# A language-model tower with a two-way state-space block: the convolution's third tap shared between VectorE and TensorE, the projections computed in plain FP32, and the fills of TensorE's order placed anew

## The reference

```python
h = emb[x]
Q, K, V = (heads(wq, bq), heads(wk, bk), heads(wv, bv))      # p = h @ w + b
...
xz = x @ in_w.T
xh, z = jnp.split(xz, 2, axis=-1)
xp = jnp.pad(xh, ((0, 0), (D_CONV - 1, 0), (0, 0)))
xc = conv_b + sum((xp[:, k:k + L, :] * conv_w[:, k] for k in range(D_CONV)))   # D_CONV = 4 taps
xc = jax.nn.silu(xc)
proj = xc @ xproj_w.T
delta = jax.nn.softplus(dt @ dt_w.T + dt_b)
deltaA = jnp.exp(jnp.einsum('bld,dn->bldn', delta, A))
deltaBu = jnp.einsum('bld,bln->bldn', delta * xc, Bm)
h = dA * h + dBu                                             # the scan over time
y = jnp.einsum('bdn,bn->bd', h, c)
y = (y + xc * D_param) * jax.nn.silu(z)
return y @ out_w.T
```

## Time and profile before

| | |
|---|---|
| time, median of 3 runs | 3424.03 us (3408.75 to 3426.32) |
| the profiled execution | 3430.8 us |
| its span in the profile | 3429.0 us |
| TensorE busy (PE) | 3235.7 us, 94% |
| VectorE busy (DVE) | 2913.3 us, 85% |
| ScalarE busy (ACT) | 2734.0 us, 80% |
| GpSimd busy (POOL) | 1449.0 us, 42% |

### The profile page before, as it was taken

The page is one execution under the profiler, slowest core; times in us unless marked ns, Lnnn a source line. Parts: engine busy times, 40 slices in busy tenths (PEclk is TensorE's granted clock), DMA queues, the critical chain, the costliest instruction groups (busy, mean ns, idle before and its releaser), DMA issues. The chain is left out here.

```text
span 3429.0 us, 75632 instructions
## 1 busy us (share of the span) xinstructions
PE 3235.7 (94%) x26913; PEld 2179.4 (64%) x26913; DVE 2913.3 (85%) x2894; ACT 2734.0 (80%) x4665; POOL 1449.0 (42%) x1379
## 2 busy tenths in 40 slices
PE   8599999999999999977899999999999999998898
PEld 7233333333333333336799999999999999986665
DVE  4789999999979999824599999999999999999422
ACT  3078888888878888842799999999999999999344
POOL 3100000000000000000588899998888899899200
PEclk9589999999989999988999999999999999999999
DMA  8420312112020200033111121211111111112431
GB/s 221 86 26 5 43 18 30 24 23 35 11 42 6 38 9 5 5 81 111 39 51 63 63 69 63 69 51 63 63 63 63 66 66 63 57 45 99 143 116 55
DMA packets 94154, 192.81 MB, mean 56 GB/s; under 512 B 16804, under 2 KB 31940, under 8 KB 92296
## 3 DMA queue, kind: packets, MB, share of 16 engines
q1 hardware_dynamic: 82616, 174.28, 18.5%
q10 hardware_dynamic: 9680, 9.84, 0.9%
q0 software_dynamic: 1536, 4.20, 0.8%
HBM read 136.64 MB, written 51.12 MB: 55 GB/s over the span
## 5 line engine op out<-in xcount | busy, mean ns | idle before, releaser
L1258 POOL TENSOR_TENSOR m_g<-m_hs,m_cb 128x512 f32<-128x512 f32 x1024 | 1286.0, 1287 | 175.5 <-PE m_ps_y L1290 89.8
L608 DVE TENSOR_REDUCE a_mx<-a_ps_m 128x2 f32<-128x1024 f32 x1024 | 1241.5, 1223 | 85.9 <-PE a_ps_m L466 68.4
L584 ACT ACTIVATE a_probs<-a_ps_s 128x512 f32<-128x512 f32 x2048 | 1110.5, 596 | 200.1 <-PE a_ps_s L496 156.0
L1390 DVE TENSOR_TENSOR_SCAN m_hs<-m_da,m_carry,m_ps_x 128x512 f32<-128x512 f32 x768 | 930.2, 1263 | 19.8 <-issue 8.0
L466 PE MATMUL a_ps_m<-a_k,a_q 48*128 48x512 f32 x2048 | 774.9, 471 | 35.6 <-DMA a_q<-q_scr 21.2
L496 PE MATMUL a_ps_s<-a_q,a_k 50*128 50x512 f32 x2048 | 774.7, 458 | 7.7 <-ACT a_probs L584 2.9
L1347 ACT ACTIVATE m_da<-m_delta,m_a_cur 128x512 f32<-128x512 f32 x1024 | 715.2, 713 | 0.0
L503 PE MATMUL a_ps_o<-a_probs,a_v 128*32 128x256 f32 x8192 | 669.0, 399 | 8.5 <-ACT a_o L571 8.0
L1278 PE MATMUL m_ps_x<-m_ident,m_bu 128*128 128x128 f32 x4096 | 627.6, 276 | 50.5 <-DVE m_hs L1390 32.1
L1290 PE MATMUL m_ps_y<-m_ident,m_g 128*128 128x128 f32 x4096 | 616.2, 273 | 0.6 <-POOL m_g L1258 0.6
L1332 ACT ACTIVATE m_bu<-m_dut,m_bt 128x512 f32<-128x512 f32 x832 | 593.8, 714 | 15.1 <-PE m_ps_x L1278 14.8
(11 more groups left out here) (150 smaller groups left out, 2525.6 us busy)
## 6 DMA issues: line engine op xcount, KB each, us to landing
m_cb<-c_scr SPq DMA_DIRECT2D x128, 512.0 KB, 3.7
y_scr<-m_ysb SPq DMA_DIRECT2D x16, 1024.0 KB, 6.5
ffn_y<-y_scr SPq DMA_DIRECT2D x14, 1024.0 KB, 7.4
a_k<-k_scr SPq DMA_DIRECT2D x96, 128.0 KB, 6.6
a_q<-q_scr SPq DMA_DIRECT2D x96, 128.0 KB, 8.9
q_scr<-p_partsq SPq DMA_DIRECT2D x16, 512.0 KB, 3.9
k_scr<-p_partsk SPq DMA_DIRECT2D x16, 512.0 KB, 6.3
m_xn<-xn_scr SPq DMA_DIRECT2D x16, 512.0 KB, 5.0
```

The lines of the kernel that those rows point to most:

```text
L584: nc.scalar.activation(probs[:, t % PR, HEADS[j]], turned(i), ACT.Exp, scale=float(DK) ** -0.5).then_inc(exped, 1)
L608: nc.vector.reduce_max(mx[:, i:i + wide], ps_m[:, b:b + wide], AX.X).then_inc(m_maxed, 1)
L1258: nc.gpsimd.tensor_tensor(g[:, t % NG], hs[:, t % NHS], cb[:, quarter % 2, n % CQ], ALU.mult).then_inc(g_ok, 1)
L1390: nc.vector.tensor_tensor_scan(hs[:, t % NHS, rev], da[:, t % NDA, rev], ps_x[:, t % NX, rev], carry[:, n, i:i + 1] if p else 0.0, ALU.mul ...
```

## The change

Two things are changed in the projections. Products are no longer split: the weights and `p_hT` stay FP32, Q and K are 4 matmuls each and V is 8 in a chunk, and the two parts of weights and of `p_hT` and what made them (lines 209, 238 and 243) are gone. And the loop is a loop again: TensorE transposes a chunk, waits for ScalarE's copy, and does Q, K and V; it no longer turns chunk n + 1 between K and V of chunk n.

In the state-space block, channel tiles 0 and 2 keep the third tap on VectorE, and for tiles 1 and 3 TensorE does it: their CONV fills have 12 matmuls in place of 8, and VectorE's in-place instruction is left out for them. The tap matrices are 24 in place of 16. All the tables of slots are written anew.

```diff
-WEIGHT_STEPS = [(0, 0, 0), (0, 0, 1), (1, 0, 0), (1, 0, 1), (0, 1, 0), (0, 1, 1)]
...
-        w_parts = [sb(f"p_wp{n}", [P, PARTS, KD, D], F32R) for n in "qkv"]
-        hT = sb("p_hT", [P, 2, PARTS, KD, CH], F32R)
+        hT = sb("p_hT", [P, 2, KD, CH], FP32)
...
+                for b, c, n, buf in chunks(pe):
+                    pe.wait_ge(rows_in[buf], (n - buf) * 32 + 64)
                     pe.wait_ge(ht_ok, ONE + n)
                     for t in range(4):
                         for k in range(KD):
                             last = nc.tensor.transpose(ps_t[:, k, t * P:(t + 1) * P],
                                                        rows[:, buf, t, k * P:(k + 1) * P], ident[:, :])
...
                     pe.wait_ge(ht_ok, ONE + n + 1)
                     for a in range(2):
                         pe.wait_ge(parts_ok[a], ONE + n)
                         for m in range(KD):
-                            last = products(ps_qk[a][:, m], lambda i, k: w_parts[a][:, i, k, m * P:(m + 1) * P],
-                                            lambda i, k: hT[:, buf, i, k], WEIGHT_STEPS)
+                            for k in range(KD):
+                                last = nc.tensor.matmul(ps_qk[a][:, m], w_sb[a][:, k, m * P:(m + 1) * P],
+                                                        hT[:, buf, k], start=k == 0, stop=k == KD - 1)
                         last.then_inc(mm_done[a], 1)
-                    if n + 1 < B * NC:
-                        turned(n + 1)
...
             def _(act):
...
+                for b, c, n, buf in chunks(act):
                     act.wait_ge(ht_ps, ONE + n + 1)
+                    nc.scalar.activation(hT[:, buf], ps_t[:, :, :], ACT.Copy).then_inc(ht_ok, 1)
...
+VECTOR_TAP = (0, 2)
...
-        taps = sb("taps", [P, 2, ND, DC - 2, P], FP32)
+        taps = sb("taps", [P, 2, ND, DC - 1, P], FP32)
...
-                 CONV + 2: (-17, -17, -17, -17, -17, -17, -17, -15), CONV + 3: (-15, -15, -15, -15, -15, -15, -15, -15),
+                 CONV + 3: (-14, -14, -14, -13, -13, -13, -13, -13, -13, -13, -13, -13),
...
-                back = k + 2
+                back = k + (2 if dt in VECTOR_TAP else 1)
...
+            if dt in VECTOR_TAP:
+                before = HB + 1 if z else HB - 1
+                nc.vector.scalar_tensor_tensor(out=ps_a[:, f % NA], in0=xh[:, dt, before:before + CH], scalar=conv_w[:, z, dt, DC - 2:DC - 1],
+                                               in1=ps_a[:, f % NA], op0=ALU.mult, op1=ALU.add).then_inc(tapped, 1)
+                nc.vector.wait_ge(tapped, s * len(VECTOR_TAP) + VECTOR_TAP.index(dt) + 1)
...
-                    for tap in range(DC - 2):
+                    for tap in range(DC - 1):
```

More of the change, by code:

```diff
@@ L144, in _ @@
                 identity(nc.gpsimd, ident[:, :], cleared, ident_ok)
-                pool.wait_ge(ids_ok, ONE + 1)
-                for n in range(B * NC):
-                    buf = n % 2
-                    if n >= 2:
-                        pool.wait_ge(ht_ps, ONE + n - 1)
-                    nc.gpsimd.tensor_copy(ids_c[:, buf], ids_t[:, n * 4:n * 4 + 4]).then_inc(ids_copied, 1)
+                for b, c, n, buf in chunks(pool):
+                    pool.wait_ge(rows_free, ONE + n + 1)
+                    pool.wait_ge(ids_ok, ONE + 1)
+                    nc.gpsimd.tensor_copy(ids_c[:, buf], ids_t[:, bass.ds(n * 4, 4)]).then_inc(ids_copied, 1)
                     pool.wait_ge(ids_copied, ONE + n + 1)
+                    pool.nop(nofuse=True)
                     for t in range(4):
@@ L171, in turned @@
                                                        rows[:, buf, t, k * P:(k + 1) * P], ident[:, :])
-                    last.then_inc(ht_ps, 1)
-                def products(out, stationary, moving, steps):
-                    for i, (part_s, part_m, k) in enumerate(steps):
-                        last = nc.tensor.matmul(out, stationary(part_s, k), moving(part_m, k), start=i == 0, stop=i == len(steps) - 1)
-                    return last
-                pe.wait_ge(ids_ok, ONE + 1)
-                turned(0)
-                pe.wait_ge(w_low, ONE + 3)
-                for n in range(B * NC):
-                    buf = n % 2
+                            if t == 3 and k == KD - 1:
+                                last.then_inc(ht_ps, 1)
+                    pe.wait_ge(ht_ps, ONE + n + 1)
+                    pe.sem_inc(rows_free, 1)
                     pe.wait_ge(ht_ok, ONE + n + 1)
@@ L188, in _ @@
                         for m in range(KD):
[L189 to L190 removed]
+                            for k in range(KD):
+                                last = nc.tensor.matmul(ps_qk[a][:, m], w_sb[a][:, k, m * P:(m + 1) * P],
+                                                        hT[:, buf, k], start=k == 0, stop=k == KD - 1)
                         last.then_inc(mm_done[a], 1)
[L192 to L193 removed]
                     pe.wait_ge(v_ok, ONE + n)
                     for t in range(4):
[L196 to L197 removed]
+                        for k in range(KD):
+                            last = nc.tensor.matmul(ps_v[:, t], hT[:, buf, k, t * P:(t + 1) * P], w_sb[2][:, k],
+                                                    start=k == 0, stop=k == KD - 1)
                     last.then_inc(v_mm, 1)
@@ L234, in _ @@
                 nc.vector.tensor_copy(ids_t[:, :], ps_t[:, 0, 0:NI]).then_inc(ids_ok, 1)
-                def turned_low(n):
-                    dve.wait_ge(ht_high, ONE + n + 1)
-                    nc.vector.tensor_tensor(hT[:, n % 2, 1], ps_t[:, :, :], hT[:, n % 2, 0].bitcast(FP32), ALU.subtract).then_inc(ht_ok, 1)
                 dve.wait_ge(w_in, ONE + 96)
-                for w in range(3):
-                    dve.wait_ge(w_high, ONE + w + 1)
-                    nc.vector.tensor_tensor(w_parts[w][:, 1], w_sb[w][:, :, :], w_parts[w][:, 0].bitcast(FP32), ALU.subtract).then_inc(w_low, 1)
-                turned_low(0)
-                for n in range(B * NC):
-                    b, c, buf = n // NC, n % NC, n % 2
+                for b, c, n, buf in chunks(dve):
                     for a in range(2):
```

63 lines of the change are left out of this document (24 added, 39 removed).

## The result

The kernel after took 3437.4 us in the median (3420.6 to 3460.3), against 3416.8 for the kernel before in the same comparison: ratio 1.0067, 95% interval 1.0051 to 1.0083. By the ratio that is 23 us slower, 17 to 28; the two medians lie 20.6 us apart.

What follows compares the result with a forecast made beforehand. VectorE and TensorE, both nearly full, were taken to bound the state-space step, TensorE the projections. Terms 23.5 + 1.6 + 2.0 + 3.9 = +31.0 us gave a median of 3455 us, range 3430 to 3476.

Steps and rivals of the forecast that it cites:

- The case that I held likeliest: Whole kernel: the forecast's own case, a median between 3445 and 3465 us, chance 0.52.
- Projections, +23.5: Projections: a chunk takes 12.52 us for 9.27, +22.75 from first K to last, and the first K ends 0.7 later.
- Tap matrices, +1.6: Building the tap matrices: eight more at 0.20 us on VectorE, all on the path since TensorE waits, +1.6 us.
- First two convolutions, +2.0: Two convolutions ahead of the stream: VectorE waits for TensorE tile by tile, +2.0 us, between 0 and 3.6.
- The stream, +3.9: The other 14 state-space steps: +0.23 us in each of ten, +0.4 in each of four without carry, +3.9 us.
- The sum of stretches: State-space step: TensorE's time in slots where it has more to do plus VectorE's elsewhere, 95.7 us before, 96.0 after.
- The sign that I named for the step: State-space step: VectorE's idle time ahead of scans in slots 50 to 8 grows by 1.5 to 2 us.
- the other signs: Profile after: Q to Q 12.5 us, TensorE idle some 1.1 us before Q, 32 third-tap instructions left.
- VectorE stays the bound: State-space step: TensorE takes the added matmuls into its gaps, 21.6 us won, +5.5 in all, 3430 us; chance 0.20.
- TensorE becomes the bound all through: State-space step: TensorE's added matmuls all count, 25.1 us lost, +52.2 in all, 3476 us; chance 0.15.
- The tables fit better: State-space step: new slots bring it to TensorE's 92.5 us plus 0.4, 46 us won, 3405 us; chance 0.05.
- Attention's clock: Attention's start: full 2.4 GHz at once would win up to 24 us, 3431; a longer 1.2 GHz stretch costs; chance 0.08.

## Why the prediction was right, and where it wasn't

**Time.** 3455 was forecast. The ratio puts the kernel at 3447 from the 3424.0 that the forecast started from, +23 us where +31.0 was forecast; the profiled execution was forecast at 3461.8 and took 3455.7. The case that I held likeliest (3445 to 3465) is the one that happened, by a narrow margin: the ratio's interval gives 3441 to 3452, and the median of the kernel's own executions is 3437.4. For the block its mechanism was wrong. By the marks the four terms are 24.6 + 1.6 + 3.6 - 8.6 = +21.2 us: the first two hold, the third is short by what the tables cost there, and the stream's has the wrong sign and is what the sum is too high by. The two last errors, 1.6 us too little and 12.5 too much, partly cancel. Of the 24.9 us between the profiled executions the other 3.7 lie in stretches without changed work, and that they are so few is luck: attention alone differs by up to 28 us between traces with the same work.

**Projections, +23.5.** Measured +24.6. Chunk to chunk 12.57 us for 12.52; an FP32 instruction of 512 columns (27.71 - 24.28) / 8 = 0.43, as taken from the feed-forward block; copy and hand-overs 1.11 us ahead of Q. From the first K's end to the last K's it is 88.01 us for 64.88, so the seven chunks brought 23.1 us for 22.75, and the first K ended at 27.88 for 26.45, +1.4 where I had +0.7: Q started at 18.10 for 17.88, and took 2.64 us more than later ones, where I had 2.2. The 0.5 us a chunk that I left open for a loop's branch isn't there. By the four passes of the Trainium skill (FP8 and Floating Point Precision, TensorE Precision Notes), taken as four times an fp32r matmul, it would have been 8 us more, an estimate. The rows say 0.86 us for 0.25, 3.5 times. Four passes still agree with this trace, only not with that base: at a granted clock of 1.00, 2.4 GHz, 0.858 us are 2059 periods, 4.0 for each of the 512 columns, while the fp32r matmul's 0.247 us are 1.16 a column and not 1.

**Tap matrices, +1.6.** Measured 1.6.

**First two convolutions, +2.0.** Here +3.6 stands between the first XH and the first scan. 1.8 is the convolutions' own: four tiles of one took 7.1 us for 6.2, twice. Another 2.2 are the new places: last convolution to first scan 11.3 us for 9.1, and 11.3 too in the kernel with new places and all taps on VectorE; 0.4 are won in between. I had priced the tap there and not the tables.

**The stream, +3.9.** It became -8.7 (first scan's start to the last one's, 1521.6 to 1512.9). Two errors of different kinds:

The steps at the ends. I took the first step for one like the others. By the prices, less 0.057 us a scan for the missing carry and without gates, VectorE has 87.2 us of work in it, and 11.2 us are waits, of which 2.47 in one piece, ended by TensorE, which in turn waited for ScalarE (TensorE's timelines, before and after):

```profile
1676.67 0.39 PE L888 MATMUL m_ps_a<-m_ident,m_proj 16*128 16x16 f32 x4 [2.72 <-ACT m_proj L928]
```

```profile
1705.08 0.42 PE L858 MATMUL m_ps_a<-m_ident,m_proj 16*128 16x16 f32 x4
```

BT waits for ScalarE's copy of PROJ, which the old table put in slot 8 and the new one in slot 6; that wait is gone. VectorE's waits in this step fell from 11.2 to 7.7 us, its work by 1.5, so 5.1 were won; the waits in slots 6 and 10, 2.7 us together, went with it, and by which entry of the tables was not taken apart. 2.2 of the 5.1 are lost again ahead of the first scan (the point above). The fourteenth step, with no XH, won 2.4.

The steady step. The sum of stretches gave 96.0 (+0.23 over its own 95.7 for before) and the trace shows 96.0 in both kernels. That is within what I had called right, but no proof of the sum. The step that failed is "I use this sum for the change": the sum had been matched to one number, 96.17, and had two engines in it. For the tap left out it gives 94.5 (measured 95.9), for new places with all taps on VectorE 96.2 (96.9), for the tap left out at new places 95.2 (95.3). It is 0.1 to 0.7 off at the new places and 1.4 off for the tap left out at the old ones: 0.8 of that is ScalarE's chain, which has no term in it. With the tap on TensorE at the old places it is off the other way. Summed from that kernel's tables, with the boundaries where TensorE's excess is largest (slots 43 to 10), it gives some 95.8, an estimate, and the step took 97.7. Why TensorE's 1.79 us count in full there stays open. The sign that I named for the step also came only in part: VectorE's waits in slots 51 to 8 grew by 0.6 us a step, not by 1.5 to 2, and by 0.8 elsewhere; the other signs, Q to Q, the idle time ahead of Q and the 32 instructions left of the third tap, came.

**The rivals.** "VectorE stays the bound": the most contended engine by occupancy is VectorE, and relieving it of 1.54 us brought 0.1. By this rival the stream would have won 21.6 us; it won 8.7, 7.5 of them in the first and the fourteenth step. The rule of the Trainium skill (Perfetto Trace Analysis, Identifying the Most-Contended Engine) didn't hold at the old places; at the new ones VectorE's part was worth 1.6 and it did. "TensorE becomes the bound all through": no, slots 0 to 43 didn't move. "The tables fit better": in the first step they do. In the steady step the new places cost 0.9 us with the tap on VectorE and win 0.6 with nobody doing it and 1.7 with TensorE doing it, which is not what a whole win needed. Attention's clock: the granted clock is 0.50 in its first stretch again, 74.5 us of it in the window of the kernel after, with a second stretch at 0.50 a little later:

```profile
122.50:197.00 74.50, 42.47 (x121) 16.12 (x125) 60.96 (x51) 6.43 (x14) 13.78 (x9) 0.50 0.46 60
197.00:214.00 17.00, 14.44 (x136) 5.15 (x132) 13.36 (x12) 11.57 (x23) 0.00 (x0) 0.98 0.94 110
215.00:255.00 40.00, 40.00 (x225) 12.88 (x225) 22.71 (x21) 20.65 (x40) 0.45 (x1) 0.50 0.01 1
```

The kernel before has two as well, 95.6 us at the start and 37.5 us later. Attention's duration is the same within 0.2 us, and this rival did not come to pass; that is luck and not a property of the change. The two traces have 143 and 140 us at 0.50 in attention. Over all fourteen traces, from 82 to 150 us of it, attention lasts, from the last K's end, 1344 us plus 0.43 us for each of them, within 2.3 us (a straight line through the fourteen, from 1377.6 to 1406.0 us), so a microsecond at half clock costs more than the 0.25 that I had estimated.

## What to carry to other kernels

Cut the steady step into stretches at instructions that both kernels have, and count every engine's busy time in each one: an engine that is not the fullest over the step (here ScalarE) may be first in the stretch that decides. Where two chains end at the same place, relief of one shows nothing, and a sum that reproduces the old time proves no mechanism; it has to be tried on kernels with one piece of work left out, at old and new places, and with two left out together. And the price of an instruction belongs to its place: the same matmuls cost 1.8 us a step in one table and 0.7 in another, and the same VectorE instructions were worth 0.1 and 1.6.
